# When the weights of an expert are requested: behind the landing of an earlier expert's scatter-additions

## The reference, cut to what matters

```python
xn = layernorm(x)                        # x: 4 x 2048 tokens of 512
x + attention(xn) + moe(xn)

# attention: random features, 8192 tokens
weights = rfs(input_weights); feats = rfs(xn)
einsum('bsr,or->bso', feats, weights)

# moe: sigmoid scores, best 4 of 8 groups, best 8 of 64 experts, at most 256 tokens an expert
g = einsum('ech,ehi->eci', dispatch, gate_w)     # 64 experts, 512 -> 256
u = einsum('ech,ehi->eci', dispatch, up_w)       # 512 -> 256
expert_out = einsum('eci,eih->ech', silu(g) * u, down_w)   # 256 -> 512
output = zeros.at[tidx].add(expert_out[...] * weight)
output = output + (silu(tokens @ shared_gate_w) * (tokens @ shared_up_w)) @ shared_down_w
```

## Time and profile before

| | us |
|---|---|
| median of the three runs | 1291.22 (1290.9 to 1291.5) |
| the profiled execution's own time | 1295.88 |
| its span, first to last instruction | 1294.1 |
| TensorE busy in it | 1269.8 (98%) |
| VectorE / ScalarE / GpSimd busy | 930.5 / 648.2 / 421.5 |
| the 16 DMA engines, mean busy share over the second half but its end | about 1.04 |

### The profile page before, as it was taken

How to read it: one execution, slowest core, us unless ns; L and a number is a source line. 1 busy time by engine, 2 the same in 40 slices (tenths; PEclk the granted TensorE clock), 3 DMA queues, 4 the chain that set the end, 5 groups by cost and what they waited for, 6 DMA issues and landing times.

```text
span 1294.1 us, 23005 instructions
## 1 busy us (share of the span) xinstructions
PE 1269.8 (98%) x7577; PEld 1118.6 (86%) x7577; DVE 930.5 (72%) x1853; ACT 648.2 (50%) x1130; POOL 421.5 (33%) x344
## 2 busy tenths in 40 slices
PE   8999999999999999999999999999999999999993
PEld 7888888888888888888889999999999999999993
DVE  7887787867878678785655777777777777777771
ACT  6422223222232223322255777777777777777771
POOL 1000000000000000000013666666666667677753
PEclk9999999999999999999999999999999999999997
DMA  8246654575545755446447999999999999999995
GB/s 309 85 137 153 135 132 113 143 168 115 133 111 145 168 107 137 112 116 136 137 132 211 297 288 302 290 299 293 298 289 297 293 293 284 299 290 301 286 250 66
DMA packets 204777, 263.66 MB, mean 204 GB/s; under 512 B 41012, under 2 KB 131016, under 8 KB 204744
## 3 DMA queue, kind: packets, MB, share of 16 engines
q1 hardware_dynamic: 175272, 191.40, 51.5%
q0 software_dynamic: 28672, 71.32, 24.5%
q10 hardware_dynamic: 800, 0.53, 0.2%
HBM read 178.18 MB, written 71.39 MB: 193 GB/s over the span
## 4 chain that ended last, share of the span: by engine, by line
PE 91%; POOL 3%; issue 3%; DVE 1%; DMA 1%; ACT 0%; POOLq 0%; ACTq 0%
PE pmm L1344 17%; PE pmm L1343 17%; PE pmm L1342 16%; PE pout L1342 11%; PE pout L1344 11%; PE pout L1343 11%; PE ptr L1599 4%; PE plp L1407 2%; POOL out_dram L1758 2%; POOL xbuf L1748 1%; PE pmm L1617 1%; PE ptr L1354 1%; DMA out_dram<-xbuf,slot_cols 1%; PE plp L1436 1%; PE plp L1416 1%
## 5 line engine op out<-in xcount | busy, mean ns | idle before, releaser
L1344 PE MATMUL pmm<-xt_hi,proj_lo 128*128 128x256 f32 (+1 forms) x768 | 241.2, 314 | 0.0
L1343 PE MATMUL pmm<-xt_lo,proj_hi 128*128 128x256 f32 (+1 forms) x768 | 241.1, 314 | 0.0
L1344 PE MATMUL pmm<-xt_hi,sgu_lo 128*128 128x256 f32 (+1 forms) x764 | 240.1, 314 | 0.0
L1343 PE MATMUL pmm<-xt_lo,sgu_hi 128*128 128x256 f32 (+1 forms) x764 | 240.1, 314 | 0.0
L1342 PE MATMUL pmm<-xt_hi,proj_hi 128*128 128x256 f32 (+1 forms) x736 | 232.5, 316 | 0.0
L1342 PE MATMUL pmm<-xt_hi,sgu_hi 128*128 128x256 f32 (+1 forms) x732 | 231.3, 316 | 0.0
L1742 POOL TENSOR_TENSOR earlier<-earlier,chosen 128x64 bf16<-128x64 bf16 x64 | 24.2, 378 | 611.4 <-DVE chosen L976 607.7
L1748 POOL DMA_INDIRECT xbuf<-rows,slot_cols x128 | 165.6, 1294 | 85.7 <-issue 37.4
L569 ACT ACTIVATE feat<-pmm,ab 128x512 f32<-128x512 f32 x66 | 45.4, 689 | 286.4 <-PE pmm L1344 286.4
L1343 PEld LDWEIGHTS pmm<-xt_lo,proj_hi 128*128 128x128 f32 x768 | 144.2, 188 | 11.2
L1343 PEld LDWEIGHTS pmm<-xt_lo,sgu_hi 128*128 128x128 f32 x764 | 143.4, 188 | 11.2
(11 more groups left out here) (220 smaller groups left out, 2640.1 us busy)
## 6 DMA issues: line engine op xcount, KB each, us to landing
raw<-in_L_ffn_gate_w_dram SPq DMA_DIRECT2D x64, 512.0 KB
raw<-in_L_ffn_up_w_dram SPq DMA_DIRECT2D x64, 512.0 KB
raw<-in_L_ffn_down_w_dram SPq DMA_DIRECT2D x64, 512.0 KB
outs<-in_L_attn_x_dram SPq DMA_DIRECT2D x32, 512.0 KB, 3.7
out_dram<-outs SPq DMA_DIRECT2D x32, 512.0 KB, 3.1
xbuf<-in_L_attn_x_dram SPq DMA_DIRECT2D x52, 256.0 KB, 8.1
raw<-xn SPq DMA_DIRECT2D x52, 256.0 KB, 6.5
rows<-raw SPq DMA_DIRECT2D x39, 256.0 KB, 4.8
```

The costliest lines, as they stand in the source:

```text
L1343: pe.matmul(psum, lh, rl, start=False, stop=False)
L1344: ins = pe.matmul(psum, ll, rh, start=False, stop=final and n == len(pairs) - 1)
```

## The change

SP asks for the weights in another order and later. The function `refill_gate_up(e)` is split into `refill_half(e, m, source)`, and a new `refill(e)` first waits until the scatter-additions of expert e-5 and all before it have landed (`added` at 32 times e-4), then requests gate of e, down of e-2 and up of e. The waits for the places in `raw` are kept. For expert 4 the new wait does not exist (its value would be zero). The first pass of the loop is written out, so that it can leave that wait away. The loads of the look-up chunks stand at the same place between the refills, behind one every four experts. At the end down of 62 and of 63 are requested. No other engine's program is changed.

```diff
-            def refill_gate_up(e):
-
-                for m, source in enumerate((gate_w, up_w)):
-                    sp.wait_ge(egu_hi_made[m], e.n - 1)
-                    sp.wait_ge(egu_lo_made[m], e.n - 1)
-                    load_half(e.b, m, source[e.n])
+            def refill_half(e, m, source):
+
+                sp.wait_ge(egu_hi_made[m], e.n - 1)
+                sp.wait_ge(egu_lo_made[m], e.n - 1)
+                load_half(e.b, m, source[e.n])
...
-            refill_gate_up(turn(3))
-            refill_down(turn(2))
-            with sp.Fori(0, CHUNKS - 3) as m:
+            def refill(e):
+
+                at_least(sp, added, 16 * CB * e.prev().prev().prev().prev().n)
+                refill_half(e, 0, gate_w)
+                refill_down(e.prev().prev())
+                refill_half(e, 1, up_w)
+
+            refill_half(turn(3), 0, gate_w)
+            refill_half(turn(3), 1, up_w)
+            for k in range(CHUNK):
+                refill(turn(CHUNK + k))
+                if k == 1:
+                    load_chunk(3)
+            with sp.Fori(1, CHUNKS - 3) as m:
                 for k in range(CHUNK):
-                    e = Turn(2 * m + 2 + k // 2, k % 2, k // 2)
-                    refill_gate_up(e)
-                    refill_down(e.prev())
+                    refill(Turn(2 * m + 2 + k // 2, k % 2, k // 2))
                     if k == 1:
                         load_chunk(m + 3)
             for n in range(E - 2 * CHUNK, E):
-                refill_gate_up(turn(n))
-                refill_down(turn(n - 1))
+                refill(turn(n))
+            refill_down(turn(E - 2))
             refill_down(turn(E - 1))
```

## The result

| | before | after |
|---|---|---|
| median, us | 1291.36 (1290.9 to 1293.36, 4 runs) | 1366.67 (1365.3 to 1368.36, 4 runs) |
| ratio after / before | | 1.0582, 95% interval 1.0569 to 1.0595 |
| the profiled execution's own time, us | 1295.88 | 1368.01 |
| its span, us | 1294.1 | 1366.3 |

The kernel became 75 us slower; 1284.8 was forecast, and the range ended at 1302. The two spans differ by 72.2 us, and that is the difference explained here.

What follows compares the result with a forecast made beforehand. PE and DMA were taken as full, with lagging additions ending the kernel. Expert 59's addition at 1247.5, one cycle of 9.2, three of 7.34 gave 1278.7 against 1285.12: 6.4 us less, 1284.8 us; range 1280.5 to 1302.

Steps and rivals of the forecast that it cites:

- What bounds the kernel: PE and DMA full to 1252 us; additions, issued up to 10.7 us after ACT's scaling (lag), end the kernel.
- the forecast case: Additions keep up at a lag of 2.6 us; span 1287.7, median 1284.8 us, chance 0.59.
- When the requests go: On SP, gate of 25 goes at the landing of 897.20, 6.7 us later; down, then up follow 0.5 us apart.
- How long the weights take: DMA landing times of the three matrices: gate 3.7 to 5.4 us, down 5.1 to 8.4, up 6.6 to 11.5.
- the slack of 7.8 to 8.9 us: Time down of n-2 has to land after the releasing additions before it holds up ACT.
- one loaded cycle of 9.2: Addition of expert 60 follows that of 59 by 9.2 us, the pace of additions beside weight traffic.
- I take the stall of PE as 0, because it corrects itself: PE loses 0 us: each microsecond PE is held or lag shrinks below 2.5 moves the landing earlier against ACT's need.
- the second rival: Down of n-2 late at ACT, PE waits, a ring sets about 9.6 us an expert: 1301.8 us, chance 0.25.
- The break-even: Pace per expert at which PE's slowing would use up the saved lag of 10.7 us: 9.41 us.
- The saving does not depend on that: The 6.4 us saved in the profiled execution, 4.7 above the median, also come off the median of 1291.2.
- What the lag gave: Lag of the additions held at 2.6 us at expert 59 instead of 9.7, so the end comes 6.4 us earlier.
- The first rival: Additions get no more of the DMA engines than before; expert 59's stays at 1254.6, time 1291.2 us, chance 0.16.

Runs made afterwards that it cites:

- experiment 1: Kernel after without the wait for landed additions, its new request order kept: 1290.07 us, ratio 0.9991.
- experiment 5: Kernel after, its wait replaced by one for POOL's issue of both additions of n-5, new order kept: 1289.7 us, ratio 0.9979.
- experiment 9: Kernel after with old order (gate, up, down of n-1), released by POOL's issue of the additions of n-5: 1289.72 us, ratio 0.9958.
- experiment 7: Kernel after with old order (gate, up, down of n-1), released by POOL's issue of the additions of n-4: 1293.5 us, ratio 1.0017.
- experiment 8: Kernel after with gate still at the landing of n-5, but up and down of n-1 behind the issue of n-4's additions: 1290.87 us, ratio 0.9982.
- experiment 2: Kernel after with its wait kept but the old order (gate, up, down of n-1): 1380.06 us, ratio 1.0661.
- experiment 4: Kernel after, same order, but released by POOL's issue of both additions of n-4 instead of n-5's landing: 1377.26 us, ratio 1.0652.
- experiment 10: Kernel after without the wait, new order kept, the same program as experiment 1 run again: 1297.89 us, ratio 1.0007.
- experiment 3: Kernel after, same order, waiting one expert earlier, for landed additions of n-6: median 1290.6 us, runs 1287.86 to 1348.73, ratio 0.9963.

## Why the prediction was wrong

**What bounds the kernel: right.** The additions as a chain of their own, and the lag as what ends the kernel, are what experiments 1, 5 and 9 confirm: with a lag of 0.5 to 2 us up to expert 59 the span ends at 1286.8 to 1287.9, as the forecast case had it (1287.7).

**When the requests go: right.** SP's burst stands at the landing, in the order and at the spacing assumed (0.55 us instead of 0.5).

**How long the weights take: right within its bounds.** The medians over all experts, from the page:

```profile
raw<-in_L_ffn_gate_w_dram SPq DMA_DIRECT2D x64, 512.0 KB, 3.6
raw<-in_L_ffn_up_w_dram SPq DMA_DIRECT2D x64, 512.0 KB, 8.9
raw<-in_L_ffn_down_w_dram SPq DMA_DIRECT2D x64, 512.0 KB, 5.2
```

The bounds were 3.7 to 5.4 for gate, 5.1 to 8.4 for down, 6.6 to 11.5 for up. Gate's 3.6 is just below its bound. Against the slack of 7.8 to 8.9 us, down with 5.2 should never have been late.

**The step that failed: the term "one loaded cycle of 9.2" for the additions, kept as it was before.** The cycle was taken from rows in which the weights were asked for one by one, 2.7 and 3.5 us apart, and its upper value of 9.95 came from that same kernel. No row of before shows a burst ahead of an addition, and what a row doesn't show should have been bounded the way the weights' landing was; the additions' was not. Measured it is 10.56, above the worst value considered: the additions' first packet comes after 4.8 us instead of 2.6. Experiments 7 and 8 against experiment 2 show what makes it so: three matrices requested ahead of the additions, instead of none or one. From it also follows why down was late after all: the slack was counted with a lag of 2.5 us and a turn of 9.3 between expert 20's issue and its landing. With a lag of 4.9 (expert 20: issued at 909.43, scaled by 904.56) and a turn of 10.4 (to 919.81) the burst goes out 3.5 us later against ACT. Of 7.8 to 8.9 us, 4.3 to 5.4 are left for a matrix that takes 5.2.

**The second: "I take the stall of PE as 0, because it corrects itself".** The correction is real: a PE that is held moves the landing earlier against ACT's need, and the lag doesn't grow past 8.7 us. But it is read in the wrong direction. Two paces are coupled, that of PE (9.22 us an expert) and that of the additions (10.56), and what couples them, down that comes late, holds the faster one back to the slower. PE's 48.5 us of gaps are that. The ring that the second rival drew (landing, weights, products, scaling, addition, landing) is not the path in the kernel after: from the landing of expert 17, which releases the burst of 888.07, to the scaling of expert 20 and on to its landing at 919.81 it takes 31.8 us, but 4.9 of them expert 20 spends scaled and waiting for the additions before it. The path is the three additions in a row. A ring does set the pace in experiment 4, two experts long and with the additions' landing not in it. The break-even that the prediction itself worked out, 9.41 us an expert, was passed by 1.15.

**The third: how a late load reaches PE.** The prediction looked at ACT's program only. What stands behind the waiting split in DVE's program is the look-up work, and PE's 32.6 us are charged to it. The chunk loads, the only part of the look-up that the prediction costed, are waited for nowhere in the trace.

**From the profiled execution to the median: wrong too.** "The saving does not depend on that" took 6.4 us off a median of 1291.2. The profiled execution was a long one, 4.7 us above the median, with a lag of 10.3 us at the end; experiment 10's profile is that of a long execution with a large lag, experiment 1's that of a short one with a small lag. The forecast span was met by experiments 5 and 9 (1287.9 and 1287.8 against 1287.7), but their medians are 1289.7, not 1284.8, and no run of any kernel here is below 1287.78. So the forecast median was out of reach even where its mechanism held. How large the lag was in before's shorter runs was not profiled.

**What the lag gave: right in kind, smaller in size.** The lag at expert 59 fell from 9.7 to 4.5 us instead of to 2.6, and at expert 63, where it ends the kernel, from 10.3 to 8.3.

**The rivals.** "Weights come too late, and PE waits" named the place where PE is held (ACT at down of n-2, on one engine in order), and it had 0.25. But it took the lateness as the cause, where in the kernel after the additions' slower turn comes first; and its pace of 9.6 was put at the middle of two values neither of which had a burst in it. Its formula with 10.56 gives 56 x (10.56 - 9.22) = 75 us; that only restates the measured pace and is no test of it. As a cause of its own it is what experiment 4 shows. The first rival, that the additions get no more than before, is refuted on the other side: they got less. The rule of the Trainium skill behind it (DMA: Bandwidth & Descriptors, "Queues, rings and completion order") was read there to mean that further requests in one queue take nothing more from the other. That conclusion fails here: the first packet comes after 3.5 us with one matrix requested ahead and after 4.8 to 5.7 with three. The rule itself, about engines that have work in both queues, is not refuted by that, since the traces don't show from when on the engines had the additions' packets to choose from; once those have started they are moved no slower than before (5.0 us against 5.9).

**What stays open.** The delay lies in the start of an addition and not in its transfer, but whether it arises before its packets reach the DMA engines or in their choice between the queues is not shown. Nor is why a kernel without the wait sometimes runs into a lag of 9.7 us and sometimes keeps 0.5 (experiments 1 and 10): of that only the outcome is.

## What to carry to other kernels

When a wait makes several transfers start at the event that also releases another chain, look at what that chain has to issue at the same instant: put the transfers behind its issue (here a semaphore after POOL's last descriptor work) and early enough for their users, or let only the one that is needed first go ahead. Before calling a delay "self-correcting", ask which of the two coupled paces is the slower: the correction brings the other down to it, and the price is the difference times the number of stages. Write down the ring that the wait closes as well, and look in the trace for slack in it before you call it the path. A cost measured between spread-out requests is no bound for the same requests in a burst.

## What the runs showed of the hardware

- Three requests of 512 KB sent within 1.3 us ahead of a scatter-addition (256 rows of 2 KB an expert) went with a median of 8.1 to 8.6 us from issue to landing (the kernel after, 2, 3), against 6.4 to 6.8 where the weights were requested one or two at a time (experiments 1, 5, 8, 9) and 5.7 with all three behind it (experiment 4, a slower kernel whose DMA engines move 253 GB/s instead of 293 to 295).
- All of that is in the start: the first packet of an addition came 2.1 us after the start of its issue with nothing else under way, 2.2 to 3.0 with three matrices requested behind it (experiments 4, 7), 3.4 to 3.5 with one or two at a time (1, 5, 9) or one ahead (8), 4.8 to 5.7 with three ahead (after, 3, 2).
- A mean DMA share of 0.93 did not mean that the DMA engines set the pace: around the landing looked at the share was 0.13 for one microsecond, with work for both queues left in the program. The kernel was bound by the times from request to landing.
- The gaps of PE took some of its clock with them. Behind ACT's wait of 6.29 us (columns as in rows 1):

```profile
874.00:876.00 2.00, 0.00 (x0) 0.00 (x0) 0.01 (x1) 1.09 (x2) 0.00 (x0) 1.00 1.09 314
...
878.00:880.00 2.00, 1.19 (x10) 1.19 (x11) 2.00 (x3) 0.94 (x1) 1.69 (x2) 0.50 0.91 262
880.00:882.00 2.00, 2.00 (x10) 1.90 (x9) 0.62 (x3) 1.13 (x3) 1.27 (x1) 0.50 0.97 295
...
884.00:886.00 2.00, 2.00 (x13) 1.74 (x12) 0.93 (x2) 1.22 (x2) 1.26 (x1) 1.00 1.12 261
```

  PE stood still from 873.4 to 878.8, and the granted clock was 0.50, the lower of its two levels (1.2 of 2.4 GHz), from within that gap until about 884. Over the experts the mean was 0.96 to 0.98; on the 578 us of PE's busy time that is some 19 us, an estimate. With the 48.5 us of gaps it makes 67 of the 72.4 us by which the scaling of expert 59 is late. That is an account of PE's time and not a second cause: experiment 2 has as large gaps at a mean clock of 0.99 and is slower.
- Two executions of one program differed by 17 us (spans of 1286.8 and 1304.1, experiments 1 and 10): the last expert was scaled 10.1 us later in the second, and its lag was 10.4 us instead of 2.8.
